# Keys' transposes moved behind the value products, query weights in two buffers and split a part per pair, in a decoder layer on one core

## Chip, cores and metric

The kernel runs on one core of one Trainium2 chip. Times are device microseconds (us) of an execution. The kernel before takes 2011.68 us, the median of three runs (2011.28 to 2014.92).

## What is computed

One decoder layer on x of 4 x 512 x 512, in three steps, each ending in a residual addition and a layer norm. The change touches the second one alone. Cut to that:

```python
x = _layernorm(x + attention_over_features(x, Wq, Wk, Wv, Wo))        # stage A
ln_out = _ln(x, ln_w, ln_b)                                           # stage B from here
q  = fp8_linear(ln_out, wq,  wq_scale,  q_in_scale)     # 16 heads of 128
k  = fp8_linear(ln_out, wk,  wk_scale,  k_in_scale)     # 8 groups of 128, 2 heads each
v  = fp8_linear(ln_out, wv,  wv_scale,  v_in_scale)
qx = fp8_linear(ln_out, wqx, wqx_scale, qx_in_scale)    # queries for the context
q, k, qx = _ln(q), _ln(k), _ln(qx)                      # per head, with weight and bias
core = gqa(q, k, v)                                     # softmax over 512 positions
kx, vx = split(cond @ w_kv_x.T);  kx = _ln(kx)
xout = gqa(qx, kx, vx)                                  # softmax over 64 positions
cat = fp8(concat(core, xout) / proj_smooth)
x = _layernorm(x + cat @ wproj.T * scales)
x = _layernorm(x + bitlinear_ffn(x))                                  # stage C
```

## The kernel before

Each engine has its program written out by hand, in one fixed order, and the engines meet through semaphores. Stage A runs over the 4 batches, stage C over 16 tiles of 128 rows. Stage B runs over 8 groups of heads (g) and in each over the 4 batches (b): 32 pairs, numbered n = 4g + b. A pair has four tiles (st = 0 to 3) of 128 queries, numbered T = 4n + st.

In each tile the pair function of TensorE (PE, line 483) issues: the scores of 2 heads against 512 keys (line 496), the projections of one tile of the NEXT pair n + 1 (project, line 387; next_proj, line 505), the value products of the tile before (av, line 440: lines 446 and 452), the transposes of the normalised probabilities of both heads (line 530, "PT" below), a transposition of a projected query tile (turn_q, line 422), and the output projection of the tile before last (project_out, line 455). At st 3 the keys of pair n + 1 are transposed as well (turn_k, line 428). Queries and keys are transposed into the same PSUM bank, MB; so each waits until ScalarE (ACT) has copied out what the other left there. At st 0 the context scores (line 567) use MB too.

ACT evicts PSUM and computes the exponentials: its pair (line 777) does two exps (line 786), the copies raw and KV of the projections (raw_kv, line 709), ob_out (line 769), the copies of PT (prT), qt_out (line 730) and kt_out (line 737). VectorE (DVE; pair on line 1085) adds the output projection into x1 (accumulate, line 1069), takes row maxima (line 1094), normalises heads (head_norm, line 1034), scales the probabilities (scale_rows, line 1045), gathers head statistics (head_stats), rounds to FP8 (round_terms, line 1053).

The projection weights of a group (columns Q 256, QX 256, K 128, V 128) are loaded in f32 into wst by one DMA (load_proj, line 251) and split into two f16 halves whose sum is the scaled weight: ACT writes the high half wh (split_high, line 694), DVE the low half wl (split_low, line 1004). There is one buffer of each. The last projection with a group's weights is issued at st 3 of the pair b = 2. So ACT splits K and V there behind raw_kv, Q behind that tile, and QX at st 0 of b = 3; DVE does K, V, Q and then QX at st 0 of b = 3; and PE waits on wl_ready in proj_kv and proj_q of that tile. At the start of stage B ACT and DVE split all four before PE's first projection, and DVE then quantises the last batch.

Of the kernel before, what the change touches and what calls it, by code (L numbers as in the profile page):

```python
# [25 lines left out]
P = 128  # L26
NB = 4
# [14 lines left out]
WCOL = {Q: (0, 256), QX: (256, 512), K: (512, 640), V: (640, 768)}  # L42
NW = 768
# [20 lines left out]
def build(nc, a, out):  # L64
    ctx = ExitStack()
    with ctx:
# [3 lines left out]
        def sb(stack, name, shape, dt=F32):  # L70
# [69 lines left out]
        wst = sb(stB, "wst", [P, KT, NW])  # L140
        wh = sb(stB, "wh", [P, KT, NW], F16)
        wl = sb(stB, "wl", [P, KT, NW], F16)
# [54 lines left out]
            wst_loaded wkx_loaded wpst_loaded  # L197
# [15 lines left out]
        out_stored = [sem(f"out_stored{i}") for i in range(2)]  # L213
        xt_loaded = [sem(f"xt_loaded{i}") for i in range(2)]
# [4 lines left out]
        def tern(c):  # L219
            if c < 8:  # L220
                return wgu[:, c // 2, (c % 2) * F:(c % 2 + 1) * F]
            return wdn[:, (c - 8) * 4:(c - 7) * 4, :].rearrange("p k n -> p (k n)")

# [5 lines left out]
        def _(sp):  # L229
# [52 lines left out]
            load_proj(0)  # L282
            load_context(0)
            load_out(0)
# [3 lines left out]
            load_proj(1)  # L288
            for n in range(TT):
# [39 lines left out]
        def _(pe):  # L329
# [57 lines left out]
            def project(dst, c, j, b):  # L387
                lo, hi = WCOL[c]
                for k in range(KT):
                    for m, w in enumerate((wh, wl)):  # L390
                        ins = mm(dst, XQ[:, c, k, b * S + j * P:b * S + (j + 1) * P], w[:, k, lo:hi],  # L391
                                 start=(k == 0 and m == 0), stop=(k == KT - 1 and m == 1))
                return ins

            def proj_q(n, j, b, weights=None):
                for c in (Q, QX):
                    lo, hi = WCOL[c]
                    if weights is not None:
                        pe.wait_ge(s["wl_ready"], weights + (3 if c == Q else 4))
                    ins = project(P0[:, lo:hi], c, j, b)  # L400
                ins.then_inc(s["proj_q_made"], 1)

            def proj_kv(n, part, b, weights=None):
                if 3 * n + part:
                    pe.wait_ge(s["kv_out"], 3 * n + part)
                if weights is not None:
                    pe.wait_ge(s["wl_ready"], weights + 2)
# [4 lines left out]
                for i, j in enumerate(KVPART[part]):  # L412
                    for c, lo in ((K, 0), (V, P)):
                        ins = project(P1[:, 256 * i + lo:256 * i + lo + P], c, j, b)
# [53 lines left out]
            pe.wait_ge(s["wl_ready"], 4)  # L468
            for j in range(4):
                if j:  # L470
                    pe.wait_ge(s["raw_out"], j)
                if j < 3:
                    proj_kv(0, j, 0)
                proj_q(0, j, 0)
# [8 lines left out]
            def pair(g, b, first, last):  # L483
                n = 4 * g + b
                nxt = not (last and b == 3)
                for st in range(ST):
                    T = 4 * n + st
                    if st == 0:
                        pe.wait_ge(s["kt_out"], n + 1)
                        pe.wait_ge(s["qt_out"], 4 * n + 3)  # L490
                    for h in range(2):
                        if T:
                            pe.wait_ge(s["exp_done"], 2 * T + (h - 1))
                        if st == 3 and h == 0:
                            pe.wait_ge(s["qt_out"], 4 * n + 4)
# [9 lines left out]
                    def next_proj():  # L505
                        if T >= 3:
                            pe.wait_ge(s["acc_done"], T - 2)
                        if st < 3:
                            proj_kv(n + 1, st, (b + 1) % 4)
                        pe.wait_ge(s["raw_out"], 4 * n + 4 + st)  # L510
                        proj_q(n + 1, st, (b + 1) % 4)
# [11 lines left out]
                    for h in range(2):  # L523
# [8 lines left out]
                        if h == 0 and st == 0:  # L532
                            pe.wait_ge(s["kt_out"], n + 1)
                            turn_q(n, 3)
                        if h == 0 and st and nxt:
                            if st == 1:
                                pe.wait_ge(s["xs_sub"], n + 1)
                            else:
                                pe.wait_ge(s["qt_out"], 4 * n + 4 + st - 1)
                            turn_q(n + 1, st - 1)  # L540
                        if h == 1 and st == 3 and nxt:
                            pe.wait_ge(s["qt_out"], 4 * n + 4 + 3)
                            turn_k(n + 1)
                    if st == 2 and nxt and b % 2:
                        turn_kx(n + 1)
                    if st and T >= 2:
# [5 lines left out]
                        project_out(T - 2)  # L552
                    if st == 0:
                        weights = 4 * g + 4 if b == 3 else None
                        if nxt:
# [5 lines left out]
                            else:  # L561
                                proj_kv(n + 1, 0, (b + 1) % 4)
# [7 lines left out]
                        if nxt:  # L570
                            if b % 2:
                                proj_kv(n + 1, 0, (b + 1) % 4, weights)
# [3 lines left out]
                            proj_q(n + 1, 0, (b + 1) % 4, weights)  # L576
# [81 lines left out]
        def _(act):  # L658
# [35 lines left out]
            def split_high(g, parts):  # L694

                act.wait_ge(s["wst_loaded"], 16 * g + 16)
                for c in parts:
                    lo, hi = WCOL[c]
                    for k in range(KT):
                        ins = act_f(wh[:, k, lo:hi], wst[:, k, lo:hi], ACT.Copy, scale=srel[:, c, k:k + 1])  # L700
                    ins.then_inc(s["wh_ready"], 1)
# [47 lines left out]
            split_high(0, (K, V, Q, QX))  # L749
# [27 lines left out]
            def pair(g, b, first, last):  # L777
                n = 4 * g + b
                nxt = not (last and b == 3)
                for st in range(ST):  # L780
# [9 lines left out]
                    if nxt and st in (1, 3):  # L790
                        raw_kv(n + 1, st, (b + 1) % 2)
                        if st == 3 and b == 2 and not last:
                            split_high(g + 1, (K, V))
                    if T:
                        ob_out(T - 1)
                    if nxt and st == 2:
                        raw_kv(n + 1, st, (b + 1) % 2)
                    for h in range(2):
# [4 lines left out]
                        if h == 0:  # L803
                            if st == 0:
                                qt_out(n, 3)
                            elif nxt:
# [600 lines left out]
```

## Time and profile before

| | us |
|---|---|
| median of three runs | 2011.68 |
| the profiled execution | 2012.47 |
| its span | 2010.7 |
| PE busy (share of the span) | 1809.7 (90%) |
| DVE busy | 1535.9 (76%) |
| ACT busy | 1064.5 (53%) |
| POOL busy | 263.1 (13%) |
| mean granted TensorE clock | 0.972 |

The profile is one execution, taken by the hardware profiler. The span is the time between the first and the last instruction; the execution's own time holds 1.8 us more around it. Stage A fills the span to about 365 us, stage B runs to about 1763 us, stage C to the end. Busy shares are means over these stages. The ends of matmuls are modelled: consecutive ones overlap in the rows, so what a group of them takes is read from start to start.

### The profile page before, as it was taken

How to read it: one execution, taken by the hardware profiler on the slowest of the kernel's cores; microseconds unless marked ns; L12 is line 12 of the kernel's file. 1: busy time of each engine (PE TensorE's matmuls, PEld its weight loads, DVE VectorE, ACT ScalarE, POOL GpSimd, SP SyncE). 2: the span in 40 equal slices, each digit the busy share in tenths (PEclk: the TensorE clock that was granted, in tenths of full speed). 3: DMA queues.
4: the chain of work that ended last, by engine and by line, in shares of the span. 5: the costliest groups of instructions: out<-in, count | busy, mean ns of one | idle time of the engine just before them, and what ended most of it. 6: DMA issues, size and time to landing. Idle time of an engine off the chain costs nothing.

```text
span 2010.7 us, 32238 instructions
## 1 busy us (share of the span) xinstructions
PE 1809.7 (90%) x11024; PEld 1248.2 (62%) x11024; DVE 1535.9 (76%) x4964; ACT 1064.5 (53%) x2526; POOL 263.1 (13%) x361
## 2 busy tenths in 40 slices
PE   8999999459999999989999999998999999839897
PEld 3444444337767777777777777777777777614443
DVE  0175754778887888788888788888888888788997
ACT  1121111226666666666666666666666666565555
POOL 0000000011211211111121121111211112011110
PEclk9999999769999999999999999999999999969999
DMA  5000000210011011001101101100110000420000
GB/s 210 21 0 22 0 0 0 75 61 20 17 42 41 10 42 37 21 10 41 42 17 42 42 9 42 37 21 11 39 42 17 10 10 9 176 84 16 22 22 27
DMA packets 37761, 70.78 MB, mean 35 GB/s; under 512 B 3296, under 2 KB 14048, under 8 KB 36576
## 3 DMA queue, kind: packets, MB, share of 16 engines
q1 hardware_dynamic: 37600, 68.73, 10.0%
q8 instruction: 90, 1.47, 0.3%
q14 instruction: 71, 0.58, 0.1%
HBM read 63.47 MB, written 4.19 MB: 34 GB/s over the span
## 4 chain that ended last, share of the span: by engine, by line
PE 71%; DVE 16%; ACT 9%; issue 3%; POOL 1%; DMA 0%; ACTq 0%; POOLq 0%; DVEq 0%; SPq 0%
PE bank L335 17%; PE bank L391 14%; PE bank L446 10%; PE bank L496 10%; PE bank L458 5%; PE bank L530 4%; PE bank L452 3%; PE bank L567 2%; DVE wl L1010 2%; ACT yb L774 2%; PE bank L425 2%; DVE am L1195 2%; ACT qT L733 2%; ACT hb L862 1%; ACT wh L700 1%
## 5 line engine op out<-in xcount | busy, mean ns | idle before, releaser
L391 PE MATMUL bank<-wh,XQ 128*128 128x256 f16 (+1 forms) x2048 | 355.8, 249 | 25.2 <-DVE wl L1010 24.0
L391 PE MATMUL bank<-wl,XQ 128*128 128x256 f16 (+1 forms) x2048 | 359.9, 249 | 0.0
L786 ACT ACTIVATE pr<-bank,nmx 128x512 f32<-128x512 f32 x256 | 175.8, 691 | 178.2 <-DVE nmx L1094 174.5
L496 PE MATMUL bank<-kT,qT 128*128 128x512 f32 x512 | 250.9, 613 | 0.8 <-ACT kT L739 0.7
L446 PE MATMUL bank<-prT,KV 128*128 128x256 f32 x1024 | 242.3, 379 | 0.5 <-ACT prT L662 0.4
L391 PEld LDWEIGHTS bank<-wh,XQ 128*128 128x128 bf16 x2048 | 204.0, 100 | 49.1 <-DVE wl L1010 20.1
L446 PEld LDWEIGHTS bank<-prT,KV 128*128 128x128 f32 x1024 | 189.5, 190 | 52.5 <-issue 23.0
L391 PEld LDWEIGHTS bank<-wl,XQ 128*128 128x128 bf16 x2048 | 202.9, 99 | 22.8 <-issue 10.3
L1307 POOL TENSOR_TENSOR rdev<-gvar,cst 128x7 f32<-128x7 f32 x128 | 190.5, 1488 | 10.0
L1094 DVE TENSOR_REDUCE nmx<-bank 128x1 f32<-128x512 f32 x256 | 169.5, 684 | 25.4 <-PE bank L496 22.1
L774 ACT ACTIVATE yb<-bank,rsT 128x128 bf16<-128x128 f32 x512 | 146.6, 372 | 79.0 <-PE bank L452 79.0
L1305 POOL TENSOR_TENSOR gvar<-mvB,geps 128x7 f32<-128x7 f32 x128 | 27.3, 213 | 1126.2 <-DVE mvB L1031 1126.2
L662 ACT ACTIVATE prT<-bank 128x512 f32<-128x512 f32 x256 | 157.5, 616 | 7.5 <-PE bank L530 7.5
L530 PE MATMUL bank<-identf,pr 128*128 128x128 f32 x1024 | 154.4, 274 | 6.3 <-DVE pr L1051 6.2
L662 ACT ACTIVATE raw<-bank 128x512 f32<-128x512 f32 x128 | 76.3, 596 | 154.4 <-PE bank L391 81.4
L496 PEld LDWEIGHTS bank<-kT,qT 128*128 128x128 f32 x512 | 95.0, 196 | 90.5 <-issue 64.3
L1041 DVE TENSOR_SCALAR nq<-raw,mvB,rdev 128x128 f32<-128x128 f32 x512 | 142.2, 342 | 0.7 <-POOL rdev L1307 0.7
L458 PE MATMUL bank<-wp,cq 128*128 128x512 bf16 x512 | 132.2, 381 | 2.9 <-DVE x L1071 2.9
L733 ACT ACTIVATE qT<-bank,hlq 128x256 f32<-128x256 f32 x256 | 132.7, 584 | 1.2 <-PE bank L425 1.1
L1051 DVE TENSOR_SCALAR pr<-pr,ri 128x512 f32<-128x512 f32 x256 | 124.6, 487 | 9.1
L530 PEld LDWEIGHTS bank<-identf,pr 128*128 128x128 f32 x1024 | 121.6, 142 | 14.7 <-DVE pr L1051 8.3
L614 PE MATMUL bank<-wgu,xiT 128*128 128x512 bf16 x512 | 118.5, 387 | 10.3 <-ACT hs L856 6.9
(157 smaller groups left out, 3032.0 us busy)
## 6 DMA issues: line engine op xcount, KB each, us to landing
wst<-in_wcat SPq DMA_DIRECT2D x8, 1536.0 KB, 6.8
wpst<-in_wproj SPq DMA_DIRECT2D x8, 1024.0 KB, 5.2
wa<-in_wgu SPq DMA_DIRECT2D x32, 256.0 KB, 2.6
wch<-in_wgu SPq DMA_DIRECT2D x8, 1024.0 KB, 12.1
xT<-in_xT SPq DMA_DIRECT2D x4, 1024.0 KB, 5.4
x<-in_x SPq DMA_DIRECT2D x4, 1024.0 KB, 11.9
wkx<-in_wkvx SPq DMA_DIRECT2D x8, 512.0 KB, 4.1
wa<-in_wdn SPq DMA_DIRECT2D x32, 128.0 KB, 2.6
```

What stands on the lines that cost most here:

```text
L335: ins = mm(dst, lhs(k), rhs(k), start=(k == 0), stop=(k == n - 1))
L391: ins = mm(dst, XQ[:, c, k, b * S + j * P:b * S + (j + 1) * P], w[:, k, lo:hi], start=(k == 0 and m == 0), stop=(k == KT - 1 and m == 1))
L446: mm(OB[:, 0:2 * P], KV[:, n % 2, t, P:2 * P], prT[:, st % 2, t, :, :].rearrange("p h s -> p (h s)"), start=(t == 0), stop=(t == ST - 1))
L458: ins = mm(P0[:, :], cq[:, T % 2, c * P:(c + 1) * P], wp[:, c, :], start=(c == 0), stop=(c == 3))
L496: mm(SB_[h][:], qT[:, h, st * P:(st + 1) * P], kT[:, :], start=True, stop=True).then_inc(s["scores_made"], 1)
L530: ins = nc.tensor.transpose(TB_[h][:, t * P:(t + 1) * P], pr[:, h, t * P:(t + 1) * P], identf[:])
L662: return act_f(dst, src, ACT.Copy)
L733: ins = act_f(qT[:, 2 * c:2 * c + 2, j * P:(j + 1) * P], MB[:, c * 256:(c + 1) * 256].rearrange("p (h s) -> p h s", h=2), ACT.Identity, sc ...
L774: ins = act_f(yb[:, T % 2, c * P:(c + 1) * P], OB[:, c * P:(c + 1) * P], ACT.Copy, scale=rsT[:, T // 16, c:c + 1])
L786: act_f(pr[:, h, :], SB_[h][:], ACT.Exp, bias=nmx[:, st, h:h + 1], accum_out=su[:, st, h:h + 1]).then_inc(s["exp_done"], 1)
L1094: v.tensor_reduce(nmx[:, st, h:h + 1], SB_[h][:], AX.X, ALU.max, negate=True).then_inc(s["max_ready"], 1)
L1307: g.tensor_tensor(rdev[:], gvar[:], CPOW, ALU.pow).then_inc(s["stats_ready"], 1)
```

## The change

On PE, at st 3, turn_k(n + 1) moves from behind the second PT to just behind the value products. It waits for the eviction of query tile 1, made a tile earlier, where it waited for tile 2's. The transposition of query tile 2 moves from between the two PTs to the end of the tile, behind the output projection, and waits for kt_out. ACT evicts in the same order. The scores wait for their own query tile.

wst becomes two buffers of 256 columns. A group comes in three parts (Q; QX; K and V), each by its own DMA. whq and wlq, the split query weights, exist twice (index g % 2); whk and wlk once. Parts of group g + 1 are split one per pair b = 0, 1, 2 of group g: ACT does the first half of the k tiles at st 2 and the second at st 3; DVE does the first half at the end of st 3 and the second at st 0 of the following pair. At the start of stage B the third part's DMA waits until the first part is split.

The diff, cut to its core:

```diff
-        wst = sb(stB, "wst", [P, KT, NW])
-        wh = sb(stB, "wh", [P, KT, NW], F16)
-        wl = sb(stB, "wl", [P, KT, NW], F16)
+        wst = sb(stB, "wst", [P, 2, KT, 256])
+        whq = sb(stB, "whq", [P, 2, KT, 512], F16)
+        wlq = sb(stB, "wlq", [P, 2, KT, 512], F16)
+        whk = sb(stB, "whk", [P, KT, 256], F16)
+        wlk = sb(stB, "wlk", [P, KT, 256], F16)
...
# SyncE
-            def load_proj(g):
-                if g:
-                    sp.wait_ge(s["wl_ready"], 4 * g)
-                sp.dma_start(wst[:], a["wcat"][g].rearrange("(k p) n -> p k n", p=P)).then_inc(s["wst_loaded"], 16)
+            def load_proj(part):
+                if part >= 2:
+                    sp.wait_ge(s["wl_ready"], 2 * (part - 1))
+                lo = WCOL[WPART[part % 3][0]]
+                sp.dma_start(wst[:, part % 2], ktile(a["wcat"][part // 3])[:, :, lo:lo + 256]).then_inc(wst_loaded[part % 2], 16)
...
             load_proj(0)
+            load_proj(1)
             load_context(0)
+            load_proj(2)
             load_out(0)
...
-            load_proj(1)
+            load_proj(3)
+            load_proj(4)
             for n in range(TT):
...
-                if b == 3 and g + 2 < NG:
-                    load_proj(g + 2)
                 if n + 1 < TT:
                     load_abs(n + 1)
+                if b < 3 and 3 * (g + 1) + b + 2 < 3 * NG:
+                    load_proj(3 * (g + 1) + b + 2)
...
# TensorE
                     if st == 0:
                         pe.wait_ge(s["kt_out"], n + 1)
-                        pe.wait_ge(s["qt_out"], 4 * n + 3)
...
+                    if nxt and st == 3:
+                        pe.wait_ge(s["qt_out"], 4 * n + 4 + 2)
+                        turn_k(n + 1)
...
-                        if h == 0 and st and nxt:
+                        if h == 0 and st in (1, 2) and nxt:
...
-                        if h == 1 and st == 3 and nxt:
-                            pe.wait_ge(s["qt_out"], 4 * n + 4 + 3)
-                            turn_k(n + 1)
...
                         project_out(T - 2)
+                    if st == 3 and nxt:
+                        pe.wait_ge(s["kt_out"], n + 2)
+                        turn_q(n + 1, 2)
...
# ScalarE
-                        if st == 3 and b == 2 and not last:
-                            split_high(g + 1, (K, V))
                     if T:
                         ob_out(T - 1)
+                    if nxt and st == 3:
+                        kt_out(n + 1)
...
                         if h == 1 and st == 3 and nxt:
-                            kt_out(n + 1)
+                            qt_out(n + 1, 2)
...
-                    if st == 0 and b == 3 and not last:
-                        split_high(g + 1, (QX,))
+                    if b < 3 and not last and st in (2, 3):
+                        split_high(3 * (g + 1) + b, (0, 1) if st == 2 else (2, 3))
...
-                    if st == 3 and b == 2 and not last:
-                        split_high(g + 1, (Q,))
...
# VectorE
+                    if b < 3 and not last and st == 3:
+                        split_low(3 * (g + 1) + b, 0)
                     if st == 0:
                         if T >= 2:
                             accumulate(T - 2, (4 * b - 2) % 16)
-                        if b == 3 and not last:
-                            split_low(g + 1, (K, V, Q))
+                        if b and not last:
+                            split_low(3 * (g + 1) + b - 1, 1)
...
-                        if b == 3 and not last:
-                            split_low(g + 1, (QX,))
```

How the order moves on PE, from the value products of tile 3 (line 446 before, 464 after) through the output projection to the scores of the next pair's tile 0. The operand nq is a query tile, kn the keys, pr the probabilities (PT), cq the rounded terms of the output projection. Before:

```order
L446 MATMUL bank4<-prT,KV 128x256 x4
L452 MATMUL bank4<-pxT,VB 128x128 x2
L530 MATMUL bank2<-identf,pr 128x128 x4
L425 MATMUL bank7<-identf,nq 128x128 x4
L530 MATMUL bank3<-identf,pr 128x128 x4
L431 MATMUL bank7<-identf,kn 128x128 x4
L458 MATMUL bank5<-wp,cq 128x512 x4
L496 MATMUL bank0<-kT,qT 128x512
L496 MATMUL bank1<-kT,qT 128x512
```

After:

```order
L464 MATMUL bank4<-prT,KV 128x256 x4
L470 MATMUL bank4<-pxT,VB 128x128 x2
L449 MATMUL bank7<-identf,kn 128x128 x4
L549 MATMUL bank2<-identf,pr 128x128 x4
L549 MATMUL bank3<-identf,pr 128x128 x4
L476 MATMUL bank5<-wp,cq 128x512 x4
L443 MATMUL bank7<-identf,nq 128x128 x4
L512 MATMUL bank0<-kT,qT 128x512
L512 MATMUL bank1<-kT,qT 128x512
```

The two transpositions into bank7 (MB) have changed places and stand four groups apart instead of one.

On ACT, from the sums of absolute values that close tile 2 of the pair b = 2 to the exps of the next pair (pr). Before:

```order
L767 ACTIVATE wa,asum<-wa 128x256
L786 ACTIVATE pr,su<-bank0,nmx 128x512
L786 ACTIVATE pr,su<-bank1,nmx 128x512
L662 ACTIVATE raw<-bank5 128x512
L700 ACTIVATE wh<-wst,srel 128x128 x8
L774 ACTIVATE yb<-bank4,rsT 128x128 x4
L662 ACTIVATE prT<-bank2 128x4x128
L733 ACTIVATE qT<-bank7,hlq 128x2x128 x2
L662 ACTIVATE prT<-bank3 128x4x128
L739 ACTIVATE kT<-bank7,hln 128x512
L700 ACTIVATE wh<-wst,srel 128x256 x4
L786 ACTIVATE pr,su<-bank0,nmx 128x512
```

After:

```order
L717 ACTIVATE whk<-wst,srel 128x128 x4
L805 ACTIVATE pr,su<-bank0,nmx 128x512
L805 ACTIVATE pr,su<-bank1,nmx 128x512
L680 ACTIVATE raw<-bank5 128x512
L793 ACTIVATE yb<-bank4,rsT 128x128 x4
L756 ACTIVATE kT<-bank7,hln 128x512
L680 ACTIVATE prT<-bank2 128x4x128
L680 ACTIVATE prT<-bank3 128x4x128
L750 ACTIVATE qT<-bank7,hlq 128x2x128 x2
L717 ACTIVATE whk<-wst,srel 128x128 x4
L805 ACTIVATE pr,su<-bank0,nmx 128x512
```

The eight pieces ahead of ob_out (yb) are gone; four now stand ahead of the exps of tile 3 and four ahead of those of the next pair, and the same with two larger pieces at b = 0 and 1.

On DVE, from the last rounding (cq) of tile 3 of the pair b = 2 over the row maxima (nmx) of the next pair to its first scaled probabilities (pr). Before:

```order
L1067 TENSOR_TENSOR cq<-ysum,yck 128x512
L1071 SCALAR_TENSOR_TENSOR x1<-bank5,pscale,x1 128x512
L1094 TENSOR_REDUCE nmx<-bank0 128x1
L1094 TENSOR_REDUCE nmx<-bank1 128x1
L1041 TENSOR_SCALAR nq<-raw,mvB,rdev 128x128 x4
L1049 RECIPROCAL ri<-su 128x1
L1051 TENSOR_SCALAR pr<-pr,ri 128x512
```

After:

```order
L1082 TENSOR_TENSOR cq<-ysum,yck 128x512
L1025 SCALAR_TENSOR_TENSOR wlk<-wst,srel,whk 128x128 x4
L1086 SCALAR_TENSOR_TENSOR x1<-bank5,pscale,x1 128x512
L1111 TENSOR_REDUCE nmx<-bank0 128x1
L1111 TENSOR_REDUCE nmx<-bank1 128x1
L1056 TENSOR_SCALAR nq<-raw,mvB,rdev 128x128 x4
L1064 RECIPROCAL ri<-su 128x1
L1066 TENSOR_SCALAR pr<-pr,ri 128x512
```

Four low pieces now stand ahead of the accumulation and the maxima; four more stand a little later, ahead of the context maxima (xmx), where the sixteen pieces of a group stood before. At b = 0 and b = 1 the same two places get two pieces of 256 columns each.

## Rows read from the trace of the kernel before

**Rows 1.** The profile's line of engines: busy us (share of the span), instructions.
```profile
PE 1809.7 (90%) x11024; PEld 1248.2 (62%) x11024; DVE 1535.9 (76%) x4964; ACT 1064.5 (53%) x2526; POOL 263.1 (13%) x361
```
**Rows 2.** Windows, the body of stage B: length, busy of PE, PEld, DVE, ACT, POOL; clock, DMA.
```profile
440.00:1720.00 1280.00, 1208.41 (x8744) 956.12 (x8743) 1061.80 (x3756) 814.94 (x2101) 211.88 (x253) 0.99 0.09 27
```
**Rows 3.** PE's waits from 440 to 1720 us: total us, times, longest.
```profile
PE bank L431 <- ACT qT L733: 46.4, 30, 2.3
PE bank L391 <- DVE wl L1010: 18.7, 21, 1.8
```
**Rows 4.** Timeline of PE, b = 0 to b = 1: start us, us, instruction [idle before].
```profile
635.70 0.60 PE L530 MATMUL bank<-identf,pr 128*128 128x128 f32 x4
...
636.57 0.60 PE L530 MATMUL bank<-identf,pr 128*128 128x128 f32 x4
638.49 0.66 PE L431 MATMUL bank<-identf,kn 128*128 128x128 f32 x4 [1.32 <-ACT qT L733]
...
640.02 1.98 PE L496 MATMUL bank<-kT,qT 128*128 128x512 f32 x4
...
644.01 1.03 PE L458 MATMUL bank<-wp,cq 128*128 128x512 bf16 x4
644.88 0.60 PE L530 MATMUL bank<-identf,pr 128*128 128x128 f32 x4
```
**Rows 5.** Timeline of ACT, same boundary.
```profile
631.85 0.69 ACT L786 ACTIVATE pr<-bank,nmx 128x512 f32<-128x512 f32 x1
...
635.90 1.14 ACT L774 ACTIVATE yb<-bank,rsT 128x128 bf16<-128x128 f32 x4 [1.25 <-PE bank L452]
...
639.19 0.78 ACT L739 ACTIVATE kT<-bank,hln 128x512 f32<-128x512 f32 x1 [0.26 <-PE bank L431]
```
**Rows 6.** Timeline of DVE, same boundary.
```profile
632.84 1.11 DVE L1041 TENSOR_SCALAR nq<-raw,mvB,rdev 128x128 f32<-128x128 f32 x4
...
638.52 0.43 DVE L1067 TENSOR_TENSOR cq<-ysum,yck 128x512 bf16<-128x512 bf16 x1
640.05 0.75 DVE L1071 SCALAR_TENSOR_TENSOR x<-bank,pscale,x 128x512 f32<-128x512 f32 x1 [1.11 <-PE bank L458]
...
642.04 0.69 DVE L1094 TENSOR_REDUCE nmx<-bank 128x1 f32<-128x512 f32 x1 [0.17 <-PE bank L496]
...
643.87 0.48 DVE L1051 TENSOR_SCALAR pr<-pr,ri 128x512 f32<-128x512 f32 x1
...
649.85 0.69 DVE L1113 TENSOR_REDUCE xmx<-bank 128x8 f32<-128x512 f32 x1 [1.93 <-PE bank L567]
```
**Rows 7.** Timeline of PE, turn_k at the ends of pairs 2, 3, 5, 10 and 11.
```profile
552.63 0.65 PE L431 MATMUL bank<-identf,kn 128*128 128x128 f32 x4 [2.27 <-ACT qT L733]
598.55 0.66 PE L431 MATMUL bank<-identf,kn 128*128 128x128 f32 x4 [1.32 <-ACT qT L733]
679.57 0.66 PE L431 MATMUL bank<-identf,kn 128*128 128x128 f32 x4 [1.32 <-ACT qT L733]
...
888.08 0.66 PE L431 MATMUL bank<-identf,kn 128*128 128x128 f32 x4 [2.27 <-ACT qT L733]
932.32 0.66 PE L431 MATMUL bank<-identf,kn 128*128 128x128 f32 x4 [1.32 <-ACT qT L733]
```
**Rows 8.** Windows, one us behind pair 3's waits for wl; columns as in rows 2.
```profile
570.00:571.00 1.00, 1.00 (x3) 0.54 (x2) 0.20 (x1) 0.55 (x2) 0.00 (x0) 0.50 0.78 166
```
**Rows 9.** The start of stage B: timelines of ACT, DVE, PE; a DMA line (KB each, median us).
```profile
371.92 5.64 ACT L700 ACTIVATE wh<-wst,srel 128x128 f16<-128x128 f32 x16
373.44 2.19 DVE L1010 SCALAR_TENSOR_TENSOR wl<-wst,srel,wh 128x128 f16<-128x128 f32 x8
376.00 3.27 DVE L1010 SCALAR_TENSOR_TENSOR wl<-wst,srel,wh 128x256 f16<-128x256 f32 x8 [0.37 <-ACT wh L700]
379.32 0.29 PE L391 MATMUL bank<-wh,XQ 128*128 128x128 f16 x1 [5.25 <-DVE wl L1010]
wkx<-in_wkvx SPq DMA_DIRECT2D x8, 512.0 KB, 4.1
```

More of the change, by code:

```diff
@@ L222, in tern, with split_weights, staged @@
             return wdn[:, (c - 8) * 4:(c - 7) * 4, :].rearrange("p k n -> p (k n)")
+        def split_weights(g, c, k):
+            if c in (K, V):
+                lo = WCOL[c] - WCOL[K]
+                return whk[:, k, lo:lo + P], wlk[:, k, lo:lo + P]
+            lo = WCOL[c]
+            return whq[:, g % 2, k, lo:lo + 256], wlq[:, g % 2, k, lo:lo + 256]
+        def staged(part, c, k):
+            lo = WCOL[c] - WCOL[WPART[part % 3][0]]
+            return wst[:, part % 2, k, lo:lo + WIDE[c]]
         def ktile(ap):
@@ L571, in pair @@
                             if b % 2:
[L572 removed]
+                                proj_kv(n + 1, 0)
                             if T >= 2:
@@ L691, in _, with split_high @@
             x_out(NB - 1)
[L694 to L701, printed above, removed]
+            def split_high(part, ks):
+                act.wait_ge(wst_loaded[part % 2], 16 * (part // 2) + 16)
+                for c in WPART[part % 3]:
+                    for k in ks:
+                        ins = act_f(split_weights(part // 3, c, k)[0], staged(part, c, k), ACT.Copy, scale=srel[:, c, k:k + 1])
+                ins.then_inc(s["wh_ready"], 1)
             def rows_proj(g):
@@ L748, in _ @@
             act.wait_ge(s["insc_ready"], 1)
-            split_high(0, (K, V, Q, QX))
+            for part in range(3):
+                split_high(part, (0, 1))
+                split_high(part, (2, 3))
             act.wait_ge(s["vx_cleared"], 1)
@@ L1001, in _, with split_low @@
                 ln_rows(lambda t: x1[:, b * ST + t, :], lambda t: xn[:, t, :], s["xn_ready"], True, 2 * b + 2)
-            def split_low(g, parts):
-                for c in parts:
-                    lo, hi = WCOL[c]
-                    dve.wait_ge(s["wh_ready"], 4 * g + {K: 1, V: 2, Q: 3, QX: 4}[c])
-                    for k in range(KT):
-                        ins = v.scalar_tensor_tensor(out=wl[:, k, lo:hi], in0=wst[:, k, lo:hi], scalar=srel[:, c, k:k + 1],
-                                                     in1=wh[:, k, lo:hi], op0=ALU.mult, op1=ALU.subtract)
-                    ins.then_inc(s["wl_ready"], 1)
+            def split_low(part, half):
+                dve.wait_ge(s["wh_ready"], 2 * part + half + 1)
+                for c in WPART[part % 3]:
+                    for k in (2 * half, 2 * half + 1):
+                        wh, wl = split_weights(part // 3, c, k)
+                        ins = v.scalar_tensor_tensor(out=wl, in0=staged(part, c, k), scalar=srel[:, c, k:k + 1],
+                                                     in1=wh, op0=ALU.mult, op1=ALU.subtract)
+                ins.then_inc(s["wl_ready"], 1)
             def head_stats(n, j, par):
@@ L1077, in _ @@
             own.sync()
-            split_low(0, (K, V, Q, QX))
+            for part in range(3):
+                split_low(part, 0)
+                split_low(part, 1)
             for j in range(4):
```

66 lines of the change are left out of this document (32 added, 34 removed).

## Prediction, made before the changed kernel was timed

> **What bounds the kernel now.** I read the page's engine line first: PE is busy for 90% of the span, DVE for 76% [rows 1]. The change touches stage B alone, so its body counts, 440 to 1720 us, at nearly full clock: PE 1208.4 of 1280 us, DVE 1061.8 [rows 2]. PE's 71.6 us without work are almost wholly two waits [rows 3]: turn_k for the eviction of a query tile (46.4 us, 30 times) and the projections for the low weights (18.7 us, 21 times, three in each of 7 group changes). There PE is the bound and its program is fixed, so what counts is how long PE stands still, and which new stops arise. Third I read the boundary of two pairs on all three engines [rows 4 to 6], which repeats to a few hundredths, fourth the distance of turn_k from pair to pair [rows 7], last the start of the stage [rows 9].
>
> **1. turn_k moves behind the value products.** The second PT starts at 636.57 and the next pair's scores at 640.02, 3.45 us later [rows 4]. A group of four transposes takes 0.44 us from start to start (635.70 to 636.57 is two), the output projection 0.87 (644.01 to 644.88). So 0.44 + 0.44 + 0.87 = 1.75 us of this is work and 1.70 is lost: 1.32 in the wait and the rest in the restart and a short wait of the scores for kT, whose eviction ends at 639.97 [rows 5]. At b = 2 ACT splits K and V first and the wait is 2.27 [rows 7], 0.95 more. There are 31 such places (30 in the window, one behind it), 7 of them of the longer kind: 24 x 1.70 + 7 x 2.65 = **59.4 us** off PE's path, if nothing takes its place.
>
> What must be ready in the new places: turn_k at 635.70 needs the normalised keys, out at 633.95 [rows 6], and query tile 1, evicted a tile earlier. The query tile 2 at the end needs kT out: ACT starts ob_out at 635.90 (1.14 us) and kT takes 0.78 [rows 5], so kT is out at about 637.8; PE gets there at 635.70 + 3 x 0.44 + 0.87 = 637.89. That is close. I take 0; its bounds are 0 (the sum) and 0.2 us in each of 31 pairs (ACT's start-up once more), 6 us. The scores' own wait is one for a tile evicted long before: nothing.
>
> **2. The group change.** From turn_k to turn_k the pair b = 3 takes 598.55 - 552.63 = 45.92 us, the like pair b = 1 without a change 679.57 - 638.49 = 41.08 [rows 4, 7]. Extra: 4.84. Five of the seven are like this one, two are shorter (932.32 - 888.08 = 44.24, extra 3.16): together **30.2 us**. 18.7 of it is the wait; the other 11.5 is TensorE at half clock after it: 0.50 granted at 570 us [rows 8], 1.2 of 2.4 GHz, after a stretch in which PE had stopped three times. With two buffers Q and QX are split a pair ahead or more. K and V have one buffer; their last low pieces are out ahead of xmx at b = 3. DVE idled 1.93 us before xmx at b = 1 [rows 6], and PE's projection with K and V comes after the context scores for which DVE waits there, so the four pieces of 2.19 / 8 = 0.27 us (1.1 together) fit. I take the whole 30.2. The bounds are 30.2 and, if the K and V pieces come late by all of their 1.1 us, 22.5.
>
> **3. The split pieces in their new places.** Work is the same: 16 pieces per group on ACT (5.64 us in all) and on DVE (2.19 + 3.27) [rows 9]. Four places:
> - ACT, end of tile 2, ahead of the exps. The exp started at 631.85 without idle before it, so two pieces of about 0.4 us (four of 0.3 for K, V) delay it: it ends at 633.4 to 633.8 in place of 632.5. DVE asks for it after nq, at 633.95 [rows 5, 6]. Covered, with 0.2 to 0.5 us left.
> - DVE, end of tile 3, ahead of accumulation and maxima. Before, DVE idled 1.11 us there [rows 6], but for the output projection, which is now out at 637.9. The rounding ends at 638.9, then two low pieces (3.27 / 8 = 0.41 each, 0.82), the accumulation 0.7, the first maximum 0.65, and from the second maximum to the first scaled probabilities 644.35 - 642.04 = 2.31: 643.4. PE reaches the transposes that need them at 637.89 + 0.44 + (644.88 - 640.02) = 643.2. So PE waits 0.2 us, with the restart 0.3; at b = 2, with 1.1 us of pieces, 0.6. **+1.2 us per group, 8.4 in 7 groups.** Without pieces (b = 3 to b = 0) DVE has 0.6 us to spare. Bounds: 0 (the idle time shown swallows it), and all the low pieces of a group's first halves, 2.7 us, 19 in all.
> - ACT, end of tile 3: behind qT, free again at about 640.5; the first maximum is out at 641.1. Covered.
> - DVE, tile 0, ahead of xmx: 0.8 to 1.1 us in an idle time of 1.93 (less in the pair b = 2, where 16 small matmuls stand in place of kvx). Taken as 0.
>
> **4. Loads.** Each wst load of 1.5 MB becomes three of 0.5 MB. In steady state the next one is issued about two pairs, 80 us, before ACT reads it. SP's queue blocks on the split at tile 0, and copy_vx behind it waits for work of the same tile anyway; the loads of wa, wpst and wkx are needed a tile 2 or a group later. Nothing. At the start of the stage it is different. Now DVE has all low halves at 379.27 and PE begins at 379.32 [rows 9]. After: ACT's first two pieces are out at 372.7, DVE's four of Q at about 374.5; only then the third part is issued. A load of this size and row length lands in 4.1 us [rows 9]: 378.7. ACT's and DVE's pieces of K and V follow in halves, 1.2 + 1.2 + 1.1 us: 382.3. DVE's quantisation, which bounds the next 50 us, and PE start **3.0 us later**. Bounds: 1.5 (the load lands in 2.6, as a small one does) and 5.5 (the output weights' 1 MB, issued right behind, slow it).
>
> Here a rule speaks against the change. The row says 4.1 us for 0.5 MB. The Trainium skill (page "DMA: Bandwidth & Descriptors", section "Bandwidth") advises batches of 1 MiB or more for three quarters of the peak; its fit of a fixed 2.0 us and the bytes at 436 GB/s would give 3.2 us for this load, an estimate by which the start would cost 2.1 us and the sum be 1933; three loads are slower than one by either, but the queue has the time.
>
> **The sum.** 2012.5 (the profiled execution, 0.8 above the median of the runs) - 59.4 - 30.2 + 8.4 + 3.0 = 1934.3. The rest of the program is the same work: **1934 us**.
>
> **Rivals.**
> - *DVE turns late at the pair's boundary.* DVE's share of the stage rises from 83% to some 88% (1061.8 us of about 1205); if the first halves push the maxima until PE waits as long as before (1.70) at all 21 boundaries with pieces, that is 35.7 in place of 8.4: 1962 us. For it: the chain of 643.4 against 643.2 has no slack. Against it: it is 0.2 us late, not 1.7, and the idle time before xmx lets DVE catch up.
> - *The stop in MB only moves.* The last query tile waits for kT as turn_k did for qT, 1.70 us in 31 pairs; the 0.95 x 7 and the group changes are still won: 2012.5 - 6.7 - 30.2 + 8.4 + 3.0 = 1987. Against it: ACT has nothing between ob_out and kT, and four groups of PE's stand between turn_k and turn_q in place of one.
> - *Slower: the split pieces land on the path, in series, and the clock falls.* ACT has no idle ahead of the exps of tile 3. If all pieces count (11.1 us per group, 78 in 7) each of 21 boundaries gains 3.7 us of stops; before, 2.7 us of stops were followed by 11.5 / 7 = 1.65 us lost at half clock, so 21 x 1.65 = 35 comes on top: 2012.5 - 89.6 + 78 + 35 + 3 = 2039. It decides from 89.6 / 21 = 4.3 us per boundary on. Against it: of the pieces gathered in one place only 5.3 of 11.1 us reached the path (4.3 in the group change, 0.95 at turn_k).
> - *No gain:* PE's stops hide a bound of another engine just behind; 2012. DVE's 17% idle speaks against it.
>
> On the third: 23 stops of 1.32 us, one a pair, left the mean clock of the stage at 0.99 [rows 2, 3], which I take for small stops doing no harm. The Trainium skill ("TensorE: Matmul & The Clock Gate", section "A second HAM failure mode: psum-queue depth-cycling") tells of a kernel whose clock kept swinging because PE idled briefly between groups; by it even the 0.3 us stops would cost clock, and that is part of this rival's chance.
>
> **Numbers.** Forecast 0.83, DVE late 0.10, the stop moves 0.04, no gain 0.01, slower 0.02. Everything won and only the least start gives 2012.5 - 89.6 + 1.5 = 1924; all upper bounds in the forecast together give 1934 + 6 + 7.7 + 10.6 + 2.5 = 1961, and together they are unlikely; I take **1922 to 1956**, which leaves the two middle rivals out. A measurement of this kernel tells 0.2%, 4 us, from no change: faster 0.97, same 0.01, slower 0.02.
>
> **What would show it.** PE's waits from 440 us on: turn_k's gone, none at the projections, a new one of about 0.3 us at PT of tile 0 for DVE's pr, at b = 1, 2, 3 and not at b = 0; if it is over 1 us, the first rival holds. From turn_k to turn_k some 38.3 us (b = 0) and 39.5 to 40 (b odd), b = 3 like b = 1; clock 1.00 throughout. A wait at line 443 for kT means the second rival. PE's first projection at about 382 us. I am wrong if PE's waits in the body sum to over 30 us, or if PE's busy time there grows.

## The result, and the profile of the changed kernel

The changed kernel takes **1931.97 us**, the median of four runs (1931.51 to 1933.11). Beside them the kernel before took 2011.48. The ratio is 0.9602, with a 95% interval of 0.9585 to 0.9618: 4.0% faster, clear of the 0.2% that can be told from no change. The forecast was 1934 in a range of 1922 to 1956. The profiled execution took 1932.42 us, its span is 1930.6: 80.1 us shorter than before.

The page's line of engines, which answers to [rows 1]:

```profile
PE 1790.4 (93%) x11024; PEld 1245.1 (64%) x11024; DVE 1525.8 (79%) x4964; ACT 1052.5 (55%) x2526; POOL 262.9 (14%) x361
```

The instructions are as many as before on every engine. Of the 80.1 us, 60.8 came out of PE's idle time and 19.3 out of its busy time, 1809.7 before: the same instructions run shorter where no stop stands before them and where the clock isn't halved (the account is behind the sum, below). The body of stage B in the windows view (columns as in [rows 2]), and PE's waits in it, which answer to [rows 3]:

```profile
445.00:1600.00 1155.00, 1146.32 (x8446) 918.78 (x8446) 1016.26 (x3629) 777.80 (x2037) 204.85 (x245) 1.00 0.10 29
```

```profile
PE bank L518 <- DVE px L1142: 5.9, 15, 0.4
PE bank L549 <- DVE pr L1066: 2.1, 7, 0.3
```

PE is busy for 99% of this stretch, where it was 94% before, and the clock is 1.00. The waits of turn_k (46.4 us) and for the low weights (18.7 us) are gone. Two are left: one for the context probabilities px at every second pair, which the kernel before had too (6.3 us in 16 places from 440 to 1720 us), and one that is new, seven times 0.3 us, for DVE's pr. The timeline of PE at the end of the pair b = 2 of group 0, to be read against [rows 4]:

```profile
550.52 0.60 PE L449 MATMUL bank<-identf,kn 128*128 128x128 f32 x4
550.96 1.04 PE L549 MATMUL bank<-identf,pr 128*128 128x128 f32 x8
551.83 1.03 PE L476 MATMUL bank<-wp,cq 128*128 128x512 bf16 x4
552.70 0.60 PE L443 MATMUL bank<-identf,nq 128*128 128x128 f32 x4
553.13 1.88 PE L512 MATMUL bank<-kT,qT 128*128 128x512 f32 x4
...
557.02 1.03 PE L476 MATMUL bank<-wp,cq 128*128 128x512 bf16 x4
558.35 0.66 PE L549 MATMUL bank<-identf,pr 128*128 128x128 f32 x4 [0.30 <-DVE pr L1066]
```

From the first row to the scores, 2.61 us, there is no stop: keys, both PTs, output projection, query tile 2, scores. The stop is in the last row. The output projection starts at 557.02 and takes 0.87 us; the PT could start at 557.89 and starts at 558.35, 0.46 late. At b = 0 and b = 1 the same distance is 1.07 and 1.06 us instead of 0.87: PE loses 0.2 us there, too little for the view to name a wait. Why it is late, on DVE and, in the second block, on ACT:

```profile
553.34 0.42 DVE L1082 TENSOR_TENSOR cq<-ysum,yck 128x512 bf16<-128x512 bf16 x1
553.69 1.13 DVE L1025 SCALAR_TENSOR_TENSOR wlk<-wst,srel,whk 128x128 f16<-128x128 f32 x4
554.74 0.74 DVE L1086 SCALAR_TENSOR_TENSOR x<-bank,pscale,x 128x512 f32<-128x512 f32 x1
555.40 1.28 DVE L1111 TENSOR_REDUCE nmx<-bank 128x1 f32<-128x512 f32 x2
...
557.81 0.49 DVE L1066 TENSOR_SCALAR pr<-pr,ri 128x512 f32<-128x512 f32 x1
...
563.38 0.69 DVE L1132 TENSOR_REDUCE xmx<-bank 128x8 f32<-128x512 f32 x1 [1.00 <-PE bank L585]
```

```profile
547.70 0.71 ACT L805 ACTIVATE pr<-bank,nmx 128x512 f32<-128x512 f32 x1
...
551.74 0.80 ACT L756 ACTIVATE kT<-bank,hln 128x512 f32<-128x512 f32 x1
...
554.25 1.32 ACT L717 ACTIVATE whk<-wst,srel 128x128 f16<-128x128 f32 x4
556.11 0.69 ACT L805 ACTIVATE pr<-bank,nmx 128x512 f32<-128x512 f32 x1 [0.54 <-DVE nmx L1111]
```

DVE runs without a gap from the rounding (cq) over the four low pieces, the accumulation and the maxima to the scaled probabilities at 558.30, and PE waits for that. ACT waited 0.54 us for DVE's maximum, so its own pieces cost nothing. kT was out at 552.54, PE asked for it at 552.70: the slack was 0.16 us. PE's first projection, forecast for about 382 us, came at 383.82. Ahead of xmx 1.00 us of idle time is left on DVE with four low pieces already in it.

### The profile page after: what moved, and what is told of

Same layout as the page of the kernel before. It is cut to its first block, busy times and chain, and to the rows that moved or that the text cites. A ratio compares the mean times of both kernels' runs of the same rounds, so it can differ in the third digit from the quotient of the medians.

```text
span 1930.6 us, 32318 instructions
## 1 busy us (share of the span) xinstructions
PE 1790.4 (93%) x11024; PEld 1245.1 (64%) x11024; DVE 1525.8 (79%) x4964; ACT 1052.5 (55%) x2526; POOL 262.9 (14%) x361
## 4 chain that ended last, share of the span: by engine, by line
PE 75%; DVE 16%; ACT 5%; issue 2%; DMA 1%; POOL 1%; DVEq 0%; POOLq 0%; ACTq 0%; SPq 0%
PE bank L354 17%; PE bank L410 16%; PE bank L464 10%; PE bank L512 9%; PE bank L549 5%; PE bank L476 5%; PE bank L585 3%; PE bank L470 3%; PE bank L443 3%; DVE am L1212 2%; PE bank L437 1%; ACT hb L877 1%; PE bank L632 1%; DVE hh L1207 1%; ACT hs L871 1%
## 5 line engine op out<-in xcount | busy, mean ns | idle before, releaser
L512 PE MATMUL bank<-kT,qT 128*128 128x512 f32 x512 | 242.4, 596 | 0.7 <-ACT kT L756 0.7
L410 PE MATMUL bank<-whq,XQ 128*128 128x256 f16 x1024 | 234.7, 276 | 0.0
L410 PE MATMUL bank<-wlq,XQ 128*128 128x256 f16 x1024 | 234.5, 275 | 0.0
L680 ACT ACTIVATE prT<-bank 128x512 f32<-128x512 f32 x256 | 153.1, 617 | 13.3 <-PE bank L549 13.3
L549 PE MATMUL bank<-identf,pr 128*128 128x128 f32 x1024 | 150.5, 275 | 9.2 <-DVE pr L1066 8.6
L410 PE MATMUL bank<-whk,XQ 128*128 128x128 f16 x1024 | 126.7, 221 | 9.8 <-DVE wlk L1025 8.6
L410 PE MATMUL bank<-wlk,XQ 128*128 128x128 f16 x1024 | 126.7, 221 | 0.0
```

Source lines behind the costliest of these rows:

```text
L512: mm(SB_[h][:], qT[:, h, st * P:(st + 1) * P], kT[:, :], start=True, stop=True).then_inc(s["scores_made"], 1)
L549: ins = nc.tensor.transpose(TB_[h][:, t * P:(t + 1) * P], pr[:, h, t * P:(t + 1) * P], identf[:])
L680: return act_f(dst, src, ACT.Copy)
```

## The experiments

Times are medians; the ratio is to runs of the kernel before on the same chip. The chips differ a little (the kernel before took 2011.5 to 2013.7 us), so ratios are compared.

### e1: the order of the transposes alone

The kernel before with the change's hunks for turn_k, turn_q, kt_out and qt_out; weights, loads and splits as before.

```diff
+                    if nxt and st == 3:
+                        pe.wait_ge(s["qt_out"], 4 * n + 4 + 2)
+                        turn_k(n + 1)
...
-                        if h == 1 and st == 3 and nxt:
-                            pe.wait_ge(s["qt_out"], 4 * n + 4 + 3)
-                            turn_k(n + 1)
```

> The kernel before with the new order of the keys' and queries' transposes alone; weights in one buffer, split at the group change as before. My theory (two independent stops of TensorE): turn_k's wait of 46.4 us is gone, 31 places of about 1.75 us are won and the longer one at b = 2 too; the group change stays (waits for wl 18.7 us, pairs b = 3 some 4.3 us long in the mean, clock 0.96 there); ScalarE's pieces of K and V still stand ahead of kT at b = 2, so a new wait of 0.5 to 1 us at the last query tile there. 2011.5 - 61 + 6 = 1956 us (1952 to 1962). Rival, the stop only moves (to kT or to the transposes of the probabilities at the next tile 0): 1985 to 2011 us.

Measured: 1952.42 us, ratio 0.9705 (0.9688 to 0.9721), 59.4 us off by the ratio. PE's waits from 445 to 1600 us:

```profile
PE bank L391 <- DVE wl L1013: 19.0, 21, 1.8
PE bank L501 <- DVE px L1128: 5.9, 15, 0.4
PE bank L425 <- ACT kT L741: 4.7, 7, 0.7
```

The stop of turn_k didn't move, it went. As expected the second rival's wait, for kT, stands only where ACT still has eight pieces ahead of ob_out, seven times 0.7 us. The time is 3.6 us lower than expected. From turn_k to turn_k a pair b = 0 takes 38.13 us and a pair b = 1 39.25, where it was 39.94 and 41.08 [rows 4, 7]: **1.81 us a pair**, not 1.70.

### e2: the weights alone

The changed kernel with those hunks undone.

```diff
-                    if nxt and st == 3:
-                        pe.wait_ge(s["qt_out"], 4 * n + 4 + 2)
-                        turn_k(n + 1)
...
+                        if h == 1 and st == 3 and nxt:
+                            pe.wait_ge(s["qt_out"], 4 * n + 4 + 3)
+                            turn_k(n + 1)
```

> The changed kernel with the old order of the keys' transposes: weights in two buffers and split a part per pair alone. My theory: the group change's 30.2 us are won and 0.95 x 7 = 6.7 us at turn_k of b = 2, the start costs 3.4 us, and VectorE's low pieces cost nothing, since TensorE's stop at turn_k gives it the time; turn_k's waits stay at 31 x 1.3 us. 2011.5 - 30.2 - 6.7 + 3.4 = 1978 us (1975 to 1982); clock 1.00 from 440 us on. Rival, the split pieces cost at the pair's boundary in any order (0.9 us per group or more): 1984 us or over. Rival, the clock falls even without the waits for wl: 1989 us.

Measured: 1978.53 us, ratio 0.9825 (0.9811 to 0.9840). The window from 445 to 1600 us has a granted clock of 1.00, PE's waits are those of turn_k, 36.9 us in 28 places of at most 1.3 us, and 5.8 us for px. The pairs take 39.93 and 41.06 us throughout, b = 3 (41.06) like b = 1. So the group change costs nothing any more, and the split pieces are free as long as PE stops at turn_k. By the ratios the two parts alone take off 29.5 + 17.5 = 47 thousandths, the whole change 39.8: 14 us less than their sum, with some 5 us of uncertainty. The traces name some 12 of the 14: the low pieces reach the path only when both parts are there (7.4 us, below), and in e1 three changes of group fewer lose the clock (4.7 us, last section), which e2 takes away, too. The longer stop at b = 2 is not counted twice: e2 wins it (b = 2 takes 39.93 us instead of 40.89), and e1 pays it again in the wait for kT. The other 2 us lie outside stage B's body, where no edit reaches: from the last pair's scores to the end it took 285.5 us in e1, 286.4 in e2 and before, 287.3 in the changed kernel.

### e3: the first K and V load without a wait

```diff
+        first_kv = qT[:, 0:2].rearrange("p h (k n) -> p (h k) n", n=256)
...
-                if part >= 2:
+                if part > 2:
                     sp.wait_ge(s["wl_ready"], 2 * (part - 1))
                 lo = WCOL[WPART[part % 3][0]]
+                if part == 2:
+                    sp.dma_start(first_kv, ktile(a["wcat"][0])[:, :, lo:lo + 256]).then_inc(s["kv0_loaded"], 16)
+                    return
```

> The changed kernel; the first group's K and V columns are loaded at once, into a tile that is free until then (qT), without waiting for the first part's split. My theory: VectorE's idle time of 3.98 us ahead of them at the start goes and everything behind it starts 3.3 to 3.5 us earlier: ratio to before 0.9585, 1928.5 us. Rival, VectorE's quantisation of the last batch or the load itself hides it: 1932 us, and the idle time before the first K and V pieces only moves.

Measured: 1927.60 us, ratio 0.9575 (0.9561 to 0.9589). The start, by the timelines of DVE and of the changed kernel's SP and ACT. Before, DVE:

```profile
365.16 2.44 DVE L971 TENSOR_SCALAR xn<-x,mv,rstd 128x512 f32<-128x512 f32 x4 [1.47 <-POOL rstd L1300]
...
379.18 0.48 DVE L910 TENSOR_SCALAR yb<-xL,rinsc 128x512 bf16<-128x512 f32 x1
```

Changed kernel, DVE, then SP's issue of the third part and ACT's first K and V piece:

```profile
366.20 2.44 DVE L986 TENSOR_SCALAR xn<-x,mv,rstd 128x512 f32<-128x512 f32 x4 [1.47 <-POOL rstd L1317]
...
381.46 2.31 DVE L1025 SCALAR_TENSOR_TENSOR wlk<-wst,srel,whk 128x128 f16<-128x128 f32 x8 [3.98 <-ACT whk L717]
383.68 0.48 DVE L925 TENSOR_SCALAR yb<-xL,rinsc 128x512 bf16<-128x512 f32 x1
```

```profile
375.92 0.37 SPq L270 DMA_DIRECT2D wst<-in_wcat  x1
380.15 2.44 ACT L717 ACTIVATE whk<-wst,srel 128x128 f16<-128x128 f32 x8 [3.78 <-DMA wst<-in_wcat]
```

and e3's DVE:

```profile
366.36 2.43 DVE L996 TENSOR_SCALAR xn<-x,mv,rstd 128x512 f32<-128x512 f32 x4 [1.47 <-POOL rstd L1327]
...
377.73 2.31 DVE L1035 SCALAR_TENSOR_TENSOR wlk<-qT,srel,whk 128x128 f16<-128x128 f32 x8
379.96 0.48 DVE L935 TENSOR_SCALAR yb<-xL,rinsc 128x512 bf16<-128x512 f32 x1
```

From xn, the last step of stage A, to the first quantisation (yb) DVE took 379.18 - 365.16 = 14.0 us before, 17.5 in the changed kernel and 13.6 in e3. The idle time of 3.98 us is gone and everything behind moved with it: from xn to the scores of the last pair e3 takes 3.5 us less than the changed kernel, too. (The ratios say 5.4 us, and their intervals hold 3.5.) So the start costs 3.5 us, where 3.0 were forecast.

### e4: the first low half ahead of the rounding

```diff
                     if nxt and st in (1, 3):
                         head_stats(n + 1, st, (b + 1) % 2)
+                    if b < 3 and not last and st == 3:
+                        split_low(3 * (g + 1) + b, 0)
                     if T:
                         round_terms(T - 1)
...
-                    if b < 3 and not last and st == 3:
-                        split_low(3 * (g + 1) + b, 0)
```

> The changed kernel; VectorE does the first half of the low pieces at tile 3 between the head statistics and the rounding, where it is idle for 0.73 us waiting for ob_out, instead of behind the rounding. My theory: the maxima of the next tile 0 come 0.1 us (b = 0, 1) and 0.4 us (b = 2) later than without pieces in place of 0.8 and 1.1, so TensorE's lateness at the transposes of tile 0 (0.20, 0.20, 0.46 us per group) goes: 6.0 us less, 1926 us. Rival, the lateness is not from the pieces but from the new order itself: no change, 1932 us.

Measured: 1923.55 us, ratio 0.9554 (0.9540 to 0.9569). DVE at the same boundary as above:

```profile
550.55 1.11 DVE L1025 SCALAR_TENSOR_TENSOR wlk<-wst,srel,whk 128x128 f16<-128x128 f32 x4
551.57 0.29 DVE L1072 TENSOR_SCALAR yb<-yb 128x512 bf16<-128x512 bf16 x1
...
554.02 1.28 DVE L1111 TENSOR_REDUCE nmx<-bank 128x1 f32<-128x512 f32 x2
```

The pieces run where DVE would have waited for ob_out, and counted from turn_k (550.52 above, 549.99 here) the maxima start at 4.03 us in place of 4.88. All of PE's waits for pr in the body are gone and every pair of the body takes 39.25 us (b odd) or 38.13 (b even), within 0.01. In the changed kernel they were 39.52, 38.38, 39.78 and 38.13 for b = 1, 2, 3 and 0. So the low pieces at this place cost 0.27 + 0.25 + 0.53 = 1.05 us per group, 7.4 us in seven. It is the first rival's mechanism at a fifth of its price.

### e5: the context transposes behind the projections

It aims at the wait that both kernels have: in even pairs PE waits 0.39 us at tile 1 for px.

```diff
-                    if st == 1:
-                        pe.wait_ge(s["px_scaled"], n + 1)
...
                     if nxt and st in (1, 3):
                         next_proj()
+                    if st == 1:
+                        pe.wait_ge(s["px_scaled"], n + 1)
...
+                    if nxt and st in (1, 3):
+                        raw_kv(n + 1, st, (b + 1) % 2)
                     if st == 1:
                         act.wait_ge(s["pxt_made"], n + 1)
```

> The changed kernel; at tile 1 the transposes of the context probabilities (px) move behind the next pair's projections, on TensorE, and ScalarE's copy of them behind raw and KV. It is for a version that beats both, and tests whether TensorE is the only bound left. My theory: the 16 waits of 0.39 us for px at even pairs go, with their restarts 7 us, and nothing takes their place, since the value products need the copy only behind their first four matmuls (1.7 us): ratio to before 0.957, 1925 us. Rival, VectorE or ScalarE is as near to the bound at tile 1 and raw or the value products' last part wait instead: 1930 us or more.

Measured: 1957.81 us, ratio 0.9730 (0.9717 to 0.9744): 26 us slower than the changed kernel; the rival of its expectation (1930 us or more) holds, at a price that nobody had put on it. PE's waits from 445 to 1600 us, then the timelines of ACT and PE:

```profile
PE bank L470 <- ACT pxT L679: 25.8, 29, 1.1
```

```profile
493.22 0.20 ACT L804 ACTIVATION_READ_ACCUMULATOR pr<-bank,nmx 128x1 f32 x1
494.97 0.60 ACT L679 ACTIVATE raw<-bank 128x512 f32<-128x512 f32 x1 [1.54 <-DVE nq L1055]
495.46 0.59 ACT L679 ACTIVATE KV<-bank 128x512 f32<-128x512 f32 x1
495.94 0.60 ACT L679 ACTIVATE pxT<-bank 128x512 f32<-128x512 f32 x1
...
496.60 0.71 PE L470 MATMUL bank<-pxT,VB 128*128 128x128 f32 x4 [0.69 <-ACT pxT L679]
```

raw has one buffer: ACT may overwrite it only when DVE's head_norm (nq) has read it, and stood still for 1.54 us. The copy of px, behind it in ACT's queue, was out at 496.5; PE wanted it at 495.9. The expectation had looked at what the products need and not at what stands ahead of the copy.

### e6: e3, e4 and e5 together

> The three edits of e3, e4 and e5 together on the changed kernel. My theory (each takes its own stop of TensorE away, and the stops are in series): 1932 - 3.5 - 7.4 - 7 = 1914 us, ratio to before about 0.951; no wait of TensorE left between 450 and 1600 us. Rival, they share slack of VectorE and the gains don't add: 1920 us.

Measured: 1943.56 us, ratio 0.9661 (0.9647 to 0.9674), 14 us better than e5 alone. e5's wait is unchanged (26.4 us in 30 places), and the two other edits hold their gains.

### e7: the low pieces twice

```diff
+                if part >= 3:
+                    at = 0
+                    for c in WPART[part % 3]:
+                        for k in (2 * half, 2 * half + 1):
+                            wh, wl = split_weights(part // 3, c, k)
+                            ins = v.scalar_tensor_tensor(out=junk[:, at:at + WIDE[c]], in0=staged(part, c, k), scalar=srel[:, c, k:k + 1],
+                                                         in1=wh, op0=ALU.mult, op1=ALU.subtract)
+                            at += WIDE[c]
                 ins.then_inc(s["wl_ready"], 1)
```

> The changed kernel; in the loop VectorE does each low piece twice, the second time into a tile that nobody reads. It prices the slack of the two places. My theory: at tile 3 there is none, so the second copies of the first halves (0.8, 0.8, 1.1 us per group) lengthen TensorE's wait at tile 0 by their whole length, 7 x 2.7 = 19 us; at tile 0, ahead of the context maxima, 1.0 us of idle time is left at b = 3 and about as much at b = 1, so most is swallowed, 0 to 7 us: 1951 to 1958 us, clock 1.00. Rival A, both places are on the path: 1970 us. Rival B, stops of over a microsecond bring the half clock back: 1960 us and over with a granted clock under 1.00 in the loop.

Measured: 1951.12 us, ratio 0.9698 (0.9684 to 0.9711), 19.3 us over the changed kernel by the ratios. PE's waits from 445 to 1600 us, and the window:

```profile
PE bank L550 <- DVE pr L1075: 21.2, 21, 1.4
PE bank L519 <- DVE px L1151: 7.1, 15, 0.6
PE bank L411 <- issue: 1.3, 7, 0.2
```

```profile
445.00:1600.00 1155.00, 1125.38 (x8274) 901.30 (x8273) 1033.62 (x3663) 763.47 (x2000) 199.74 (x239) 1.00 0.10 29
```

The pairs b = 1, 2, 3 take 40.31, 39.36 and 41.17 us, 3.16 us more in a group than in the changed kernel; the second copies of the first halves are 2.7 of that. So at tile 3 there is no slack, and the wait for pr grew from 2.1 to 21.2 us. At tile 0 most was swallowed: at b = 1 xmx came after an idle time of 0.47 us with four pieces ahead of it. 21 stops of up to 1.4 us, one a pair, left the clock at 1.00, so neither rival holds.

### e8: the context transposes later on PE alone

e5 with only its TensorE hunk; ScalarE keeps its order.

> The changed kernel; the context transposes move behind the next pair's projections on TensorE as in e5, but ScalarE keeps its order (copy of px ahead of raw and KV). In e5's trace raw waited for VectorE's nq and the copy of px queued behind it, 0.7 us late for TensorE in every pair. My theory: ScalarE is idle between the exps and raw (1.5 us), so the copy fits there, e5's wait goes and the 16 waits of 0.39 us for px too: 1925 us, ratio 0.957. Rival, raw comes later by the copy (0.5 us) and with it nq and the transposes of a tile further on: 1932 to 1945 us.

Measured: 1919.89 us, ratio 0.9538 (0.9525 to 0.9551), about 12.9 us off by the ratios, where 7 were expected. The waits for px are gone. A pair b = 0 takes 37.52 us in place of 38.13, 0.61 in each of 16 even pairs, 9.8 us: the restart and what the view does not call a wait cost another 0.22 us beside the 0.39. The rest of the difference lies within the intervals. The rival is answered by ACT's timeline: raw starts 2.99 us behind the first exp (492.78 and 489.79 us), as in the changed kernel (494.30 and 491.31), and waits for DVE's nq in both. The copy fits into that wait.

### e9: e3, e4 and e8 together

> The edits of e3, e4 and e8 together on the changed kernel. My theory: the three stops are in series: 1932 - 3.5 - 7.4 - 7 = 1914 us, ratio to before 0.951 to 0.952, no wait of TensorE between 450 and 1600 us. Rival, the gains share slack: 1918 us or more.

Measured: **1911.27 us**, ratio 0.9494 (0.9481 to 0.9507), the fastest of all, 1.1% below the changed kernel. The window from 445 to 1640 us:

```profile
445.00:1640.00 1195.00, 1186.96 (x8715) 962.72 (x8806) 1060.98 (x3795) 815.04 (x2131) 215.32 (x255) 1.00 0.11 36
```

From 445 to 1600 us the view names no wait of PE. Odd pairs take 39.25 or 39.26 us (one took 39.33), even ones 37.51 or 37.52. Stage B's body is now PE's own work, busy for 99% of the stretch, at a granted clock of 1.00.

## Why the prediction was right, step by step

**The bound.** It rested on PE's idle time being almost whole in two waits, 65.1 of 71.6 us, with a fixed program around it. The rest was the third wait, for px (6.3 us), which the prediction does not name; it stayed, so the sum did not need it. e1 and e2 each took one wait away and left the other as it was, but for the longer stop at b = 2. Nothing else of another engine reached PE's path, save DVE at the one place forecast; but kT was only 0.16 us from it.

**1. turn_k, forecast 59.4 us.** Right in mechanism and a little small. The pairs got shorter by 1.81 us each, and the 0.95 us at seven pairs came on top: 31 x 1.81 + 6.7 = 62.8. The missing 0.1 us a pair is in how I read the stop's end: I took the scores' start at 640.02 as the end of the stop, while the scores themselves took 1.82 us to the next row (641.84) in place of 1.72. No row names a cause for this 0.1. The slack at kT, put at 0.1 us, was 0.16, and no wait appeared.

**2. The group change, forecast 30.2 us.** All won; in e4 b = 3 takes the same 39.25 us as b = 1. How the forecast divided it was off. The two short changes had the same waits as the others (2.7 us) and no half clock, with 3.16 us of extra time: so 3.16 x 7 = 22.1 us were waits and restarts, and what the five others took beyond that (1.48 to 1.68 us each) makes 8.1 us of half clock; the forecast had 18.7 and 11.5. By e7's clock and e4's pairs nothing of either came back.

**3. The low pieces, forecast +8.4 us.** Measured +7.4: 0.27, 0.25 and 0.53 us where I had 0.3, 0.3 and 0.6. At b = 0 and b = 1, where a wait of 0.3 us was forecast, the list of waits names none; the loss shows only in the distances. It was the place named, and the chain (rounding, pieces, accumulation, maxima, scaling) is the one in the trace. The other three places were free: ACT's first pieces delayed the exps without a wait behind them, its second ones were out 0.54 us before the maximum, and e7 shows that DVE's place ahead of xmx had room.

**4. The start, forecast +3.0 us.** Measured +3.5. The load was issued at 375.9 (I had 374.5; 1.0 of the difference is a later end of stage A), and ACT's first piece followed 4.2 us later. The Trainium skill's fit ("DMA: Bandwidth & Descriptors", section "Anatomy of one DMA — SWDGE (gpsimd) path"), which is for loads issued from GpSimd while this one is on SP's queue, gave an estimate of 3.2 us for that load, from which I had worked out 2.1 us for the start; the trace decides for the row of wkx, 4.1.

**The sum.** -62.8 - 30.2 + 7.4 + 3.5 = -82.1, where the forecast had -78.2, and the span fell by 80.1. Two stretches outside the change make up the 2 us: stage A's last step came 1.0 us later in this profile (366.20 against 365.16), which isn't the change's doing, for it lies between 365.04 and 366.36 in the eleven profiles with no order by kernel; and from the scores of the last pair to the end it took 1930.6 - 1643.3 = 287.3 us against 2010.7 - 1724.3 = 286.4. So the forecast's terms were 3.9 us too small a gain, and half of that was made good by luck.

PE's busy time fell because a stop costs more than its idle time. A stop of turn_k was 1.32 us of idle and 1.81 of loss, 31 x 0.49 = 15.2; the three waits of a group change were 2.7 us and cost 3.16, 3.4 in seven; the half clock was 8.1; and the low pieces took back some 5, of whose 7.4 us only 2.1 are in the list of waits. That is 21.4 us. From the scores of the second pair to those of the last one the windows view gives 1181.0 us busy before and 1159.5 now.

**The rivals.** DVE late: the mechanism is real, at 7.4 us in place of 35.7. The stop moves to kT: e1 shows that it would, if ACT were held up ahead of ob_out by eight pieces, and then for 0.7 us. Slower through pieces on the path: e2 shows them free where PE stops at turn_k, and e7 shows the clock unmoved by stops of up to 1.4 us; the seven of 0.3 us in the changed kernel left it at 1.00, too. All three needed more delay than there was.

## What to carry to other kernels

When one engine is the bound and its program is fixed, its idle time before an instruction is a price list: each wait named there can be taken out by giving its releaser more of the bound engine's own work to hide behind, and the gain is read from start to start, since restarts and short waits (0.2 to 0.5 us a stop here) aren't in the list of waits. Work that is moved must be laid where its engine already waits for the bound one; four low pieces cost 0.53 us behind the rounding and nothing 2.6 us earlier, ahead of it. And before a step is moved on one in-order engine, look at what stands ahead of it there: the copy that hid for free behind the exps cost 26 us behind a copy that had to wait for a third engine.

## What the runs showed that I had not expected

The clock does not follow the wait alone. Three changes of group in the kernel before, each with the same three waits of together 2.7 us, in the windows view (16 us each; the clock is third from the right):

```profile
560.00:576.00 16.00, 13.33 (x109) 10.46 (x108) 14.18 (x46) 7.26 (x19) 1.68 (x2) 0.89 0.31 104
892.00:908.00 16.00, 13.33 (x106) 10.82 (x105) 14.99 (x50) 7.88 (x22) 0.20 (x1) 1.00 0.20 57
1059.00:1075.00 16.00, 13.33 (x87) 9.96 (x86) 14.49 (x48) 7.17 (x21) 0.53 (x2) 0.89 0.24 75
```

PE is busy for the same 13.33 us in each, and in two of the three the granted clock fell to 0.50, 1.2 of 2.4 GHz, for a while. In the kernel before five of seven changes lost the clock and two did not; in e1, where the three waits are the same and the stops before them differ, two of seven (pairs of 45.04 us) did and five (43.36) did not. So the loss, 1.5 to 1.7 us each, does not follow from the size and order of the stops alone. What decides it no row shows. The Trainium skill ("TensorE: Matmul & The Clock Gate", section "What's actually happening") says that a free-running monitor of activity sets the clock. Equal stops with unequal effects are what such a monitor could give, but no run here shows it.
